# A projection that lags its fusion by 20 tiles instead of 21, with the gate in three slots, one turn of both maps, spread bands and one y_lo half on GpSimd

## The reference, cut to what matters

```python
ll, lh, hl, hh = haar_dwt(x)                    # x: (8, 256, 160, 160) float32
wav = concatenate([ll, lh, hl, hh], axis=1)     # (8, 1024, 80, 80)
fused = relu(bn_eval(conv1x1(wav, fusion_w, fusion_b), ...))        # 256 channels
sp_in = concatenate([mean(fused, 1), max(fused, 1)], axis=1)
spatial_out = sigmoid(conv7x7(sp_in, sa_w)) * fused
avg_ch, max_ch = mean(spatial_out, (2, 3)), max(spatial_out, (2, 3))
ch_map = sigmoid(mlp(avg_ch) + mlp(max_ch))
projected = relu(bn_eval(conv1x1(ch_map * spatial_out, proj_w, proj_b), ...))   # 1024 channels
out = haar_idwt(projected split in four) + x
```

## Time and profile before

| | |
|---|---|
| median of 3 runs | 2391.2 us (2390.98 to 2392.24) |
| profiled execution | 2397.3 us, of which the span of the profile is 2395.4 us |
| TensorE busy | 2305.2 us, 96% |
| VectorE busy | 2134.5 us, 89% |
| ScalarE, GpSimd busy | 1089.8 us (45%), 483.3 us (20%) |
| DMA engines | 9 tenths and more from 300 us on, mean 276 GB/s |
| granted TensorE clock | 0.99 mean |

### The profile page before, as it was taken

One profiled execution on the slowest core, in us unless ns is written; L12 is line 12 of the kernel. 1 busy time (PEld: TensorE's weight loads), 2 busy tenths in 40 slices (PEclk: granted clock), 3 DMA queues, 4 the chain that ended last, 5 costly groups with the idle time before them and its releaser, 6 DMA issues. The chain is left out here.

```text
span 2395.4 us, 30247 instructions
## 1 busy us (share of the span) xinstructions
PE 2305.2 (96%) x11109; PEld 2041.8 (85%) x11109; DVE 2134.5 (89%) x2773; ACT 1089.8 (45%) x1443; POOL 483.3 (20%) x467
## 2 busy tenths in 40 slices
PE   7999999999999999999999999999999999998797
PEld 6787889888898988989898888989889898886686
DVE  7877888899888998899988999889988899889798
ACT  4445534454344544455344553445434454435332
POOL 0010111111111111111111111111111111141799
PEclk9999999999999999999999999999999999999899
DMA  5455699999999999999999999999999999989898
GB/s 186 166 180 193 193 289 278 295 299 280 286 281 282 294 273 279 294 285 297 289 283 282 301 274 292 291 274 298 276 287 291 285 301 283 281 258 281 311 342 319
DMA packets 112616, 660.54 MB, mean 276 GB/s; under 512 B 17682, under 2 KB 18772, under 8 KB 112212
## 3 DMA queue, kind: packets, MB, share of 16 engines
q1 hardware_dynamic: 85108, 480.68, 52.0%
q0 software_dynamic: 27360, 177.94, 39.8%
HBM read 448.24 MB, written 210.33 MB: 275 GB/s over the span
## 5 line engine op out<-in xcount | busy, mean ns | idle before, releaser
L542 PE MATMUL pp<-y_hi,wp_hi 128*128 128x480 f32 (+1 forms) x1792 | 672.1, 375 | 42.4 <-DVE sd L868 22.6
L542 PE MATMUL pp<-y_lo,wp_hi 128*128 128x480 f32 (+1 forms) x1792 | 667.9, 373 | 0.0
L542 PE MATMUL pp<-y_hi,wp_lo 128*128 128x480 f32 (+1 forms) x1792 | 666.4, 372 | 0.0
L633 ACT ACTIVATE x_hi<-xin 128x1920 fp32r<-128x1920 f32 (+1 forms) x224 | 420.2, 1876 | 522.1 <-PE pfs L570 463.5
L570 PE MATMUL pfs<-x_hi,wf_hi 128*128 128x480 f32 (+1 forms) x1648 | 614.2, 373 | 7.5 <-DVE x_lo L781 7.0
L570 PE MATMUL pfs<-x_lo,wf_hi 128*128 128x480 f32 (+1 forms) x1648 | 612.0, 371 | 0.0
L570 PE MATMUL pfs<-x_hi,wf_lo 128*128 128x480 f32 (+1 forms) x1648 | 611.9, 371 | 0.0
L781 DVE TENSOR_TENSOR x_lo<-xin,x_hi 128x1920 fp32r<-128x1920 f32 (+1 forms) x224 | 461.4, 2060 | 133.7 <-ACT x_hi L633 133.7
L666 ACT ACTIVATE relu<-pp,t 128x480 f32<-128x480 f32 (+1 forms) x448 | 286.8, 640 | 374.3 <-PE pp L542 371.0
L457 POOL DMA_DIRECT2D xre<-in_x_dram x190 | 166.9, 879 | 1423.9 <-DVE xre L885 1423.9
L542 PEld LDWEIGHTS pp<-y_hi,wp_hi 128*128 128x128 f32 x1792 | 339.6, 190 | 92.2 <-DVE sd L868 28.7
(11 more groups left out here) (104 smaller groups left out, 1486.7 us busy)
## 6 DMA issues: line engine op xcount, KB each, us to landing
xin<-in_x_dram SPq DMA_DIRECT2D x160, 960.0 KB, 8.2
out_dram<-xre SPq DMA_DIRECT2D x160, 960.0 KB, 6.4
xre<-in_x_dram POOLq DMA_DIRECT2D x136, 960.0 KB, 10.2
xin<-in_x_dram SPq DMA_DIRECT2D x64, 800.0 KB, 7.4
out_dram<-xre SPq DMA_DIRECT2D x64, 800.0 KB, 5.5
xre<-in_x_dram POOLq DMA_DIRECT2D x54, 800.0 KB, 9.9
xre<-in_x_dram SPq DMA_DIRECT2D x24, 960.0 KB, 7.1
sigb<-sig_scratch SPq DMA_DIRECT2D x28, 400.0 KB, 7.5
```

The lines of the kernel that those rows point to most:

```text
L542: mm = pe.matmul(pp[j][:, 0:n_px], w[:, kt, cols], y[:, s.pc, kt, 0:n_px], start=(kt == 0 and m == 0), stop=(kt == CT - 1 and m == 2))
L633: nc.scalar.activation(halves(x_hi, i, k), pairs(i, k), ACT.Copy).then_inc(xhi_ready[i], 1)
```

## The change

LAG becomes 20, with EXTRA = 6. Slots 0 to 19 only fuse, 20 to 111 do both, 112 to 131 only project, and phase LAST is 6. The eight chunks are gated in phases 2, 3 and 4, as 1+2, 1+2 and 1+1. The maxima of a tile are no longer made in its own slot but in the next one, beside the sums, in one buffer (`stats`, in ring buffer 3), turned in one transpose and reduced by two instructions (`turn`). `x_lower` of half 1 stands right behind that of half 0 where `other` differs. `bands` gives ten instructions to a slot of six rows and two to one of five, up to slot 13. `y_lo` of half 1 is made by GpSimd for every tile, from a product `y_full` that ACT makes ahead of both `y_hi`; GpSimd's subtraction waits for `x_lower` of half 1. In the last slots the fourth ring buffer is taken last instead of first, and the last half tile is added by DVE in two parts, each stored by itself.

```diff
-EXTRA = 7
+EXTRA = 6
-        GATED = {2: (0, 1), 3: (2, 3), 4: (4, 5), 5: (6, 7)}
+        GATED = {2: ((0,), (1, 2)), 3: ((3,), (4, 5)), 4: ((6,), (7,))}
         def adding(kc, i):
-            return kc + LAG < NT or kc + LAG - NT in GATED
+            return kc + LAG < NT or 2 <= kc + LAG - NT < LAST
-        tail_homes = [3] + home[-3:]
+        tail_homes = home[-3:] + [3]
...
# SyncE, body(s)
-                    if GATED[s.phase][0] == 0:
-                        load_sig(s, 0)
-                    load_sig(s, GATED[s.phase][1])
+                    for c in GATED[s.phase - 1][1] if s.phase - 1 in GATED else (-2, -1):
+                        if c + 2 < NCH:
+                            load_sig(s, c + 2)
...
-                if s.phase in GATED and s.a and GATED[s.phase][1] + 1 < NCH:
-                    load_sig(s, GATED[s.phase][1] + 1)
+                if s.phase in GATED and s.a:
+                    for c in GATED[s.phase][0]:
+                        if c + 2 < NCH:
+                            load_sig(s, c + 2)
...
# GpSimd, body(s)
+                if s.c_next and not s.next_is_first and s.a:
+                    if s.load_next:
+                        gp.wait_ge(xlo_ready[1], s.k + 2)
+                    lower(s.kn)
...
# ScalarE, upper(kc)
-                if pooled(kc):
...
+                need(act, lo_pool, kc)
+                nc.scalar.activation(y_full[:, 0:n_px], fused[:, 1, ring(kc)], ACT.Copy,
+                                     scale=ch[:, 1:2]).then_inc(y_ready, 1)
...
# VectorE
+            def turn(s):
+                block, px, n = span_of(s.k - 1)
...
+                nc.vector.tensor_tensor(stats[:, PXM:PXM + n], fused[:, 0, here], fused[:, 1, here], ALU.max
+                                        ).then_inc(mx_ready, 1)
...
+                both_maps = slice(0, PXM + blocks * GROUP)
+                nc.vector.transpose(to[:, both_maps], stats[:, both_maps]).then_inc(stats_turned, 1)
...
             def body(s):
                 if s.load_next:
                     x_lower(s.k + 1, 0)
+                if s.load_next and other(s.k) != other(s.k + 1):
+                    x_lower(s.k + 1, 1)
...
                 if s.turn and not (s.phase == 0 and s.c):
-                    turn_sums(s)
+                    turn(s)
                 if s.phase in GATED:
-                    gate(s, GATED[s.phase][0])
...
-                if s.a:
-                    channel_max(s)
...
-                if s.a:
-                    turn(s)
...
                 if s.phase in GATED:
-                    gate(s, GATED[s.phase][1])
+                    for c in GATED[s.phase][1]:
+                        gate(s, c)
```

More of the change, by code:

```diff
@@ L1 @@
+import itertools
 from contextlib import ExitStack
@@ L424, in _ @@
                 body(s)
-            store(NT - 1, 1)
+            half_px = 2 * px_of(NT - 1)
+            for n in range(2):
+                rows = slice(n * half_px, (n + 1) * half_px)
+                sp.wait_ge(last_summed, n + 1)
+                sp.dma_start(dram(out_v, NT - 1, 1)[:, rows], xre[:, home[-1], rows]).then_inc(stored[home[-1]], 16)
             for p in range(RING):
-                sp.wait_ge(stored[p], 16 * home.count(p))
+                sp.wait_ge(stored[p], 16 * (home.count(p) + (p == home[-1])))
         @block.gpsimd
@@ L478, in body @@
             def body(s):
-                if s.phase == LAST and pooled(s.kc):
+                if s.phase == LAST:
                     lower(s.kc)
@@ L592, in body @@
                 if s.c_is_first:
-                    pe.wait_ge(f_ready, CT * (LAG - 1))
+                    pe.wait_ge(f_ready, CT * (max(k for k in range(LAG) if other(k)) + 1))
                 if s.c and s.phase != LAST:
@@ L981, in body @@
                     cells(s, 0)
-                if s.c_next and not s.next_is_first and not ahead:
+                if s.c_next and not s.next_is_first:
                     lower(s.kn)
@@ L986, in body @@
                 if s.turn and not (s.phase == 0 and s.c):
-                    turn_sums(s)
+                    turn(s)
                 if s.phase in GATED:
-                    gate(s, GATED[s.phase][0])
-                if ahead:
-                    butterflies(s, 0)
-                    cells(s, 0)
-                    if s.c_next:
-                        lower(s.kn)
-                if s.load_next and other(s.k) != other(s.k + 1):
-                    x_lower(s.k + 1, 1)
-                if s.a:
-                    channel_max(s)
+                    for c in GATED[s.phase][0]:
+                        gate(s, c)
                 if s.load_next and other(s.k) == other(s.k + 1):
                     x_lower(s.k + 1, 1)
-                if s.a:
-                    turn(s)
                 if s.phase == 0:
@@ L1023, in _ @@
                 body(s)
+            g = 2 * NT - 1
+            dve.wait_ge(xre_landed[home[g]], 16 * uses(g, False))
+            dve.wait_ge(cell_ready, 2 * (g + 1))
+            for n in range(2):
+                rows = slice(n * 2 * px_of(NT - 1), (n + 1) * 2 * px_of(NT - 1))
+                x = xre[:, home[g], rows]
+                nc.vector.tensor_tensor(x, x, cell[:, g % 2, rows], ALU.add).then_inc(last_summed, 1)
 _INS = ["x"] + ["L0_conv_" + n for n in (
```

126 lines of the change are left out of this document (49 added, 77 removed).

## The result

The changed kernel takes 2410.7 us (median of five, 2407.5 to 2419.4), the kernel before 2391.5: a ratio of 1.0082, interval 1.0068 to 1.0097. It is slower by 19.2 us; 24.5 was forecast, and the time lies in the range. The profiled execution takes 2410.7 too (span 2408.9), 13.4 more than that of before, which lay 6 above its own median.

A forecast was written before the change was run, and what follows sets the result against it. TensorE's unchanged work was taken as the bound, so only its idle time and clock counted: -4.3 + 5.5 + 16 + 10 - 2.7 = +24.5 on the profiled 2397.3, 2421.8; median 6.1 under, 2415.7 us; range 2400 to 2432.

The forecast's parts named there:

- A: Early fusing slots: fewer bands a slot remove idle time and a slow stretch, half a us lost in nine slots; -4.3 us.
- B: Slot 14, transposes of image 0: they start 7.0 us behind F1 instead of 2.03; +5.0, and 0.5 at low clock.
- C: Gate of image 0, slots 16 to 18: three TensorE stops of 5.9, 6.2 and 9.3 us; +14, and +2 for clock.
- D: Six mixed gates: late GpSimd y_lo and loads make stops 2.7 us instead of 1.76, all with slow stretches; +10 us.
- E: The kernel's end: later fusion and map copy (+8.7) against a DVE slot less and GpSimd's wait gone (-7.7); -2.7 us.
- the first (the stop goes): Rival for the six mixed gates: y_lo is in time, stops and slow stretches go, -15.7 instead of +10, 2390; 12%.
- The second (loads decide): Rival: late factor loads make DVE wait 1.6 us longer twice an image, +19 with clock, 2433; 13%.
- The third (collision): Rival: GpSimd and DVE collide in gated slots, 2 us an image, +12, 2428; 7%.
- The fourth (the end gains whole): Rival for the end: add and store are fast and the map copy isn't held, -8.7, 2407; 8%.

The follow-up runs named there:

- e11: The kernel before with only the bands changed, ten instructions to a slot of six rows and two to one of five: 2387.9 us, ratio 0.9984.
- e3: The changed kernel with x_lo of half 1 moved behind the turn in slots that only fuse: 2392.3 us, ratio 0.9996.
- e5: The changed kernel with x_lo of half 1 moved behind the turn and the first chunk in slots that only fuse: 2383.4 us, ratio 0.9965.
- e2: The kernel before with only the lag changed to 20 and the gate in three slots: 2405.8 us, ratio 1.0048.
- e6: The changed kernel with a third buffer for the factors of image 0, so no load waits for a chunk of its own slot: 2409.2 us, ratio 1.0072.
- e8: The changed kernel with the copy of the last image's maps ahead of a residual's load on SyncE: 2414.0 us, ratio 1.0086.
- e1: The changed kernel with lag 21 again and two chunks in each of phases 2 to 5: 2398.9 us, ratio 1.0027.
- e7: The changed kernel with lag 21, two chunks a slot, and x_lo of half 1 behind turn and first chunks in fusing slots: 2367.2 us, ratio 0.9895.
- e4: The changed kernel with GpSimd's y_lo no longer waiting for x_lo of half 1 of the next tile: 2423.7 us, ratio 1.0123.
- e10: e7 with both halves of y_lo on VectorE again up to the last slots: 2380.7 us, ratio 0.9952.
- e12: e5 (lag 20) with both halves of y_lo on VectorE again up to the last slots: 2389.7 us, ratio 0.9995.

## Why the prediction held, step by step

The direction was right, the time 5 us under the forecast. That it came so near is partly luck. The sum was for the profiled executions, and these differ by 13.4 where it says 24.5: A gained 2.7 less than said, B and C cost 2.4 more, D 12.8 less and E 3.3 less. The timed difference is larger because the profiled execution of before lay 6 us over its median. Of the steps, B was right in its stop, A and E in their sign, C came out for a cause that isn't its own, and D was wrong in its term for the clock.

- **A, bands: -4.3, measured -1.6.** Shown by e11 and e3: the bands are worth 3.8 us where the turn stands ahead of `x_lo` of half 1. In the changed kernel turn and bands both stand behind it, and six stops of 0.60 to 1.85 replace five. The step left 4 us of stops; they sum to 6.9. Its own numbers say more than it took: 5.3 us of work where 4.3 fit is 1.0 lost in each of nine slots and not 0.5, which would have left no gain.
- **B, slot 14: +5.5 with clock, measured a stop of 7.14** where 7.0 was said. The stop is within 0.2, and so is the transpose of 960 columns, 1.18 us where the slope of two rows gave 1.17; the clock behind it fell for 10.2 us with 5.8 of work, 2.9 lost where I took 0.5.
- **C, the gate of image 0: +16.** B and C together were 21.5, and the stage is 23.9 longer: 15.8 of idle time (19 was said) and 10.3 of clock (2.5 was said), by an estimate that overshoots the stage by 2.2. The stops came at the fusions named, 7.2, 3.3 and 7.4. What failed is "Nothing but 10.5 us of TensorE covers a slot here, and three chunks with a turn are 8.6 us, where 4.3 fit". That holds only for what stands behind `x_lo` of half 1; 3.1 us lay idle ahead of it, which e5 fills. The lag's own part of this is 2.3 us (191.1 less 188.8, and 167.7 less 165.4; with the old order it is -1.0, e2); the rest, 23.4, belongs to one line moved (e5). The sentence "The third chunk's factor loads only when the first is done" described real waits (2.72 and 2.40), and e6 shows that they lay off the path.
- **D, six mixed gates: +10, measured -2.8.** The stop was said to be 2.2 and 0.5 for the load: it is 2.25, and the 0.5 didn't come. The step that failed is "all six long enough for a slow stretch in place of three". None of the six has one in this profile; in e6 and e8, the same code there, two have, 3.4 us each. So the term was not +4.4 (three stretches of 1.7 would be 5.1): the half clock of the middle costs 0 to 5.0 us in the profiles of this code (changed, e6, e8, e5), against 6.8 in the profile of before. How it splits is shown by the pairs: the lag costs 15.6 in the middle (e2 less before), 13.3 (changed less e1) or 18.0 (e5 less e7), and the rest of the change gives 16 to 18 back.
- **E, the end: -2.7, measured -6.0,** of which the lag alone gives 4.9 (e2). Slot 119 gained 7.5 (7.7 said), and the last matmul lies 2.4 nearer the end (2.3 said). The copy of the maps went out 23.8 us behind the last fusion (27 said, from 17.2), yet the two stops that it could lengthen grew only from 4.9 to 5.9 us: with the 9.7 and 10.4 my sum has +8.0 for them. The term of +8.7 for the map copy was wrong, as the load back took 4.8 us instead of 6.7 and the clock used up part of the rest. Half clock at the end cost 5.3 more, where I had -0.7.

Of the rivals, the first (the stop goes) had its place right and its condition wrong: `y_lo` came 2.25 us late, and only the slow stretches went. The second (loads decide) is refuted by e6 for image 0, and in the middle stage VectorE waits for no factor's load at all. The third (collision) does not happen in the changed kernel, where the maxima take 652 ns as in e1, and is what its wait keeps away, as e4 shows. The fourth (the end gains whole) needed a copy that isn't held; it was held, but that cost little.

Two more slips of the sums changed nothing: 3.09 us are the sums turned and one chunk (1.27 and 1.82), not two, and the +19 of the second rival would be 2434.7, not 2433.

The timed difference is 5.8 us over that of the two profiles. The middle of the same code held none, two and two half-clock stretches in three executions, and four in the profile of before; that this makes up the difference is likely and not shown.

## What to carry to other kernels

An instruction that is tied to a late event of another engine splits its engine's slack in two; count the room on each side of it, not the sum. Cost a moved line as its own edit: here the place of one instruction (27.2 us between the changed kernel and e5, 31.7 between e1 and e7) outweighed the change that it came with, and my reading of the whole laid it on the lag. And a wait in the trace is not a cost until another buffer has been tried.

## What the runs showed that I had not expected

- The clock doesn't follow the length of a stop alone. Stops of 1.12 us (e10) had no half clock behind them in six cases, those of 1.76 in three and four of six (before, e11), those of 2.25 in none, two, two, two and three of six (changed, e3, e6, e8, e5), those of 2.38 in one of three (e4), those of 2.79 in two of six (e12), those of 3.14 in five of six (e2).
- Long stops cost more than they last: 17.9 us of stops in slots 17 to 19 came with three stretches at half clock, of 10.2, 3.4 and 13.7 us. The stop of 7.14 in slot 14, which stands alone, had 10.2 us too (changed, e1, e8), or 6.8 (e4, e6).
- GpSimd and VectorE slow each other when both read two inputs from SBUF (e4 against the changed kernel): GpSimd's subtraction by 24%, VectorE's maxima of 480 columns by 76%, an `x_lo` that is met from 2.15 to some 3.3 us.
